# A fused attention and FFN kernel: the halves of the attention products are added by accumulating transfers instead of by GpSimd

## The reference

```python
x = x + _layernorm(attn(_layernorm(x), ...))
x = x + _layernorm(ffn(_layernorm(x), ...))

# attn: rows of x are seen as tokens of C = 16 channels, split in two branches of 8 channels.
# In a branch, windows of 8 tokens attend to each other:
attn = softmax(q * 8 ** -0.5 @ k.T)          # 8 x 8 for each window, hd = 8
out = attn @ v + lepe                        # lepe: 3-tap convolution of v
att = concat([x1, x2]) @ proj_w + proj_b     # then a layer norm over the 16 channels, and + token

# ffn: int8 weights (512 x 2048, 2048 x 512) with scales
gate = silu((x @ w_gate) * s_gate)
up = (x @ w_up) * s_up
y = ((gate * up) @ w_down) * s_down
```

## Time and profile before

| | us |
|---|---|
| median of 2 runs | 1000.54 (999.96 to 1001.12) |
| the profiled execution, its own time | 1001.03 |
| its span, first to last instruction | 999.3 |
| PE busy | 910.1 |
| DVE busy | 825.5 |
| POOL busy | 765.8 |
| ACT busy | 658.6 |
| mean granted clock of TensorE | 0.968 |

### The profile page before, as it was taken

The page is one execution under the profiler, slowest core; times in us unless marked ns, Lnnn a source line. Parts: engine busy times, 40 slices in busy tenths (PEclk is TensorE's granted clock), DMA queues, the critical chain, the costliest instruction groups (busy, mean ns, idle before and its releaser), DMA issues.

```text
span 999.3 us, 17730 instructions
## 1 busy us (share of the span) xinstructions
PE 910.1 (91%) x6511; PEld 705.6 (71%) x6511; DVE 825.5 (83%) x1099; ACT 658.6 (66%) x1153; POOL 765.8 (77%) x698
## 2 busy tenths in 40 slices
PE   1566499989999999999999999999999999989996
PEld 1444387767878777777777787877777787767674
DVE  2799898978898998989898998989898989894322
ACT  1876477676768768586767778586767686654431
POOL 1477686978889797989889797988899787876432
PEclk9878599999999999999999999999999999989998
DMA  7112212040311313040402213040403111120201
GB/s 202 42 43 50 76 26 60 1 128 1 87 41 44 85 22 106 1 127 1 98 30 62 66 33 95 2 128 1 127 1 77 31 43 43 23 64 19 67 11 32
DMA packets 68886, 54.94 MB, mean 55 GB/s; under 512 B 40384, under 2 KB 56768, under 8 KB 68800
## 3 DMA queue, kind: packets, MB, share of 16 engines
q1 hardware_dynamic: 63936, 53.49, 20.0%
q10 hardware_dynamic: 4864, 0.32, 0.3%
HBM read 37.02 MB, written 16.78 MB: 54 GB/s over the span
## 4 chain that ended last, share of the span: by engine, by line
PE 76%; DVE 10%; POOL 5%; issue 3%; DMA 2%; ACT 2%; SPq 1%; POOLq 0%; DVEq 0%; ACTq 0%
PE ps_up L552 21%; PE ps_gate L552 19%; PE ps_acc L571 18%; PE ps_w L513 10%; PE ps_w L533 3%; PE ps_w L504 2%; POOL sum L808 2%; DVE fst L1033 2%; DVE xr L1028 2%; PE ps_w L543 2%; DVE prod L950 1%; PE ps_w L522 1%; DMA xrow<-in_L_attn_x 1%; DVE mid L1049 1%; SPq L432 1%
## 5 line engine op out<-in xcount | busy, mean ns | idle before, releaser
L808 POOL TENSOR_TENSOR sum<-prod 128x1024 f32<-128x1024 f32 x128 | 301.7, 2366 | 46.4 <-DVE prod L950 39.2
L950 DVE TENSOR_TENSOR prod<-ps_x,qkvl 128x2048 f32<-128x2048 f32 x128 | 291.3, 2279 | 5.0 <-ACT ps_x L664 4.6
L571 PE MATMUL ps_acc<-wd,mid 128*128 128x512 f16 x1024 | 241.4, 379 | 0.0
L552 PE MATMUL ps_gate<-xhi,wg 128*128 128x256 f16 x1024 | 233.6, 275 | 3.0 <-DVE xlo L1040 3.0
L552 PE MATMUL ps_up<-xhi,wu 128*128 128x256 f16 x1024 | 232.3, 274 | 1.6 <-DVE mid L1049 1.6
L552 PE MATMUL ps_gate<-xlo,wg 128*128 128x256 f16 x1024 | 233.6, 275 | 0.0
L552 PE MATMUL ps_up<-xlo,wu 128*128 128x256 f16 x1024 | 232.1, 274 | 0.0
L732 ACT ACTIVATE mid<-ps_gate,sgate 128x256 f32<-128x256 f32 x256 | 107.1, 470 | 170.0 <-PE ps_gate L552 169.5
L876 POOL TENSOR_TENSOR mid<-mid 128x512 f16<-128x512 f32 x128 | 148.7, 1162 | 52.4 <-ACT mid L738 52.4
L1049 DVE SCALAR_TENSOR_TENSOR mid<-ps_up,sup,mid 128x256 f32<-128x256 f32 x256 | 110.1, 471 | 91.2 <-PE ps_up L552 69.2
L571 PEld LDWEIGHTS ps_acc<-wd,mid 128*128 128x128 f16 x1024 | 100.3, 98 | 96.7
(11 more groups left out here) (138 smaller groups left out, 1279.6 us busy)
## 6 DMA issues: line engine op xcount, KB each, us to landing
xrow<-in_L_attn_x SPq DMA_DIRECT2D x16, 512.0 KB, 4.5
xb<-in_L_attn_x SPq DMA_DIRECT2D x128, 64.0 KB
attn_rows<-ratt SPq DMA_DIRECT2D x32, 256.0 KB, 2.6
o<-attn_rows SPq DMA_DIRECT2D x32, 256.0 KB, 3.5
xr<-in_L_attn_x SPq DMA_DIRECT2D x16, 512.0 KB, 5.0
out_x<-y SPq DMA_DIRECT2D x15, 512.0 KB, 5.3
mid<-in_L_ffn_w_gate SPq DMA_DIRECT2D x1, 1024.0 KB, 5.4
mid<-in_L_ffn_w_up SPq DMA_DIRECT2D x1, 1024.0 KB, 8.1
```

The costliest lines, as they stand in the source:

```text
L552: mm = nc.tensor.matmul(ps[:, ROWS * i:ROWS * i + ROWS], w[:, k, P * j:P * j + P], xs[:, n % 2, k, :], start=(k == 0 and part == 0), stop= ...
L571: return nc.tensor.matmul(ps_acc[q][:], f[:, m % SPLITS, ROWS * i + P * q:ROWS * i + P * q + P], wd[:, 2 * m + i, :], start=(m == 0 and pa ...
L808: nc.gpsimd.tensor_tensor(sum4[:, u % 2, :].rearrange("p (s c) -> p s c", c=4), s[:, :, 0:4], s[:, :, 4:8], ALU.add).then_inc(half_done, 1)
L950: nc.vector.tensor_tensor(prod[:, half].rearrange("p (s j k) -> p s j k", j=WIN, k=WIN), left[:, :, None, :].broadcast_to([P, 4 * WIN, WIN ...
```

## The change

- `halve` is no longer a GpSimd addition. GpSimd issues a transfer that adds the second half of a product buffer onto the first, inside SBUF: 128 partitions, 1024 float32 (4 KB) each, so 512 KB read, 512 KB added to. Its end is signalled by the transfer's semaphore.
- For that, VectorE writes the products in another layout: the first four of each eight in the first half of the buffer, the last four in the second. The reduction reads the first half. `sum4` is gone.
- There are three product buffers (`RING = 3`). A product waits for the sum of the unit three before, no longer for the GpSimd addition of the unit two before.
- In `finish`, ScalarE copies the two accumulators out of PSUM (`finish_copy`), and GpSimd multiplies them by the scales (`finish_scale`); VectorE only takes the statistics. The last tile's `finish_last` stays as it was.
- `START`, `PLAN` and `OWN` have new contents.

```diff
-        prod = sb("prod", [P, 2, 4 * WIN * WIN * HB])
-        sum4 = sb("sum4", [P, 2, 1024])
+        prod = sb("prod", [P, RING, 2, 1024])
...
+            def finish_copy(n, bank):
+                act.wait_ge(down_done, CHUNKS * n + CHUNKS)
+                need(act, s_out, 16 * n)
+                for q in range(2):
+                    nc.scalar.activation(y[:, q, :], ps_acc[q][:], ACT.Copy).then_inc(acc_read, 1)
...
             def halve(n, u, stage):
-                pool.wait_ge(prod_done, 2 * UNITS * n + UNITS * stage + u + 1)
-                need(pool, sum_done, 2 * UNITS * n + UNITS * stage + u - 1)
-                s = prod[:, u % 2, :].rearrange("p (s c) -> p s c", c=HB)
-                nc.gpsimd.tensor_tensor(sum4[:, u % 2, :].rearrange("p (s c) -> p s c", c=4), s[:, :, 0:4], s[:, :, 4:8],
-                                        ALU.add).then_inc(half_done, 1)
+                unit = 2 * UNITS * n + UNITS * stage + u
+                pool.wait_ge(prod_done, unit + 1)
+                parts = prod[:, unit % RING]
+                pool.dma_start(parts[:, 0], parts[:, 1], accum_op=ALU.add).then_inc(half_done[unit % RING], 16)
...
+            def finish_scale(n, bank):
+                if n == 0:
+                    pool.wait_ge(scales_set, 1)
+                pool.wait_ge(acc_read, 2 * n + 2)
+                for q in range(2):
+                    nc.gpsimd.tensor_tensor(y[:, q, :], y[:, q, :], sdown[:], ALU.mult).then_inc(y_scaled, 1)
...
             def products(n, u, stage):
                 br, half = u // 2, u % 2
-                need(dve, half_done, 2 * UNITS * n + UNITS * stage + u - 1)
+                unit = 2 * UNITS * n + UNITS * stage + u
+                need(dve, sum_done, unit + 1 - RING)
...
-                nc.vector.tensor_tensor(prod[:, half].rearrange("p (s j k) -> p s j k", j=WIN, k=WIN),
+                nc.vector.tensor_tensor(prod[:, unit % RING].rearrange("p i (s k) -> p s i k", k=4),
...
             def reduce_unit(n, u, stage, dst):
-                dve.wait_ge(half_done, 2 * UNITS * n + UNITS * stage + u + 1)
-                nc.vector.tensor_reduce(dst, sum4[:, u % 2, :].rearrange("p (s c) -> p s c", c=4), AX.X,
+                unit = 2 * UNITS * n + UNITS * stage + u
+                dve.wait_ge(half_done[unit % RING], 16 * (unit // RING) + 16)
+                nc.vector.tensor_reduce(dst, prod[:, unit % RING, 0].rearrange("p (s c) -> p s c", c=4), AX.X,
                                         ALU.add).then_inc(sum_done, 1)
...
             def finish(n, bank):
-                dve.wait_ge(down_done, CHUNKS * n + CHUNKS)
-                need(dve, s_out, 16 * n)
-                for q in range(2):
-                    nc.vector.tensor_tensor(y[:, q, :], ps_acc[q][:], sdown[:], ALU.mult).then_inc(acc_read, 1)
-                dve.wait_ge(acc_read, 2 * n + 2)
+                dve.wait_ge(y_scaled, 2 * n + 2)
```

More of the change, by code:

```diff
@@ L42 @@
 TERMS = 96
+RING = 3
 Bank = namedtuple("Bank", "ps last")
@@ L194, in sandwich_kernel @@
         prod_done = sem("prod_done")
-        half_done = sem("half_done")
+        half_done = [sem(f"half_done_{i}") for i in range(RING)]
         sub_done = sem("sub_done")
@@ new lines, in sandwich_kernel @@
+        PLAN = [(-111.23, ("load_row",)), (-89.34, ("stats",)), (-86.02, ("load_xb",)), (-74.99, ("spread",)),
+                (-69.59, ("apply",)), (-66.23, ("xt", 0, 0)), (-62.34, ("xt", 0, 1)), (-61.16, ("qkv", 0, 0)),
+                (-56.61, ("qkv", 0, 1)), (-56.43, ("qkv", 0, 2)), (-55.04, ("qkv", 0, 3)), (-54.12, ("xt", 1, 0)),
+                (-53.12, ("qkv", 1, 0)), (-50.99, ("qkv", 1, 1)), (-48.63, ("xt", 1, 1)),
+                (-48.41, ("token_bias",)), (-48.19, ("qx", 0)), (-47.89, ("qkv", 1, 2)), (-44.29, ("qkv", 1, 3)),
+                (-43.63, ("qk", 0)), (-43.27, ("qx", 1)), (-40.79, ("qk", 1)), (-40.70, ("qk", 2)),
+                (-40.50, ("qk_sum", 0)), (-37.81, ("qk_sum", 1)), (-35.59, ("qk", 3)), (-35.22, ("softmax", 0)),
+                (-34.06, ("qk_sum", 2)), (-33.65, ("exp", 0)), (-32.21, ("pv", 0)), (-30.32, ("qk_sum", 3)),
+                (-30.24, ("softmax", 1)), (-29.00, ("pv_sum", 0)), (-27.30, ("exp", 1)), (-26.98, ("pv", 1)),
+                (-26.09, ("pv", 2)), (-25.60, ("att_store",)), (-25.03, ("pv", 3)), (-24.55, ("pv_sum", 1)),
+                (-22.51, ("recip",)), (-22.28, ("pv_sum", 2)), (-21.30, ("attn_out",)), (-20.25, ("pv_sum", 3)),
+                (-17.36, ("cat", 0)), (-16.74, ("cat", 1)), (-16.58, ("proj", 0)), (-16.16, ("square", 0)),
+                (-15.84, ("cent_var",)), (-15.83, ("load_xr",)), (-15.40, ("proj", 1)), (-15.01, ("square", 1)),
+                (-14.95, ("cent_std",)), (-13.82, ("cent_out",)), (-5.85, ("ffn_norm1",)), (-3.54, ("norm1_add",)),
+                (-3.00, ("ffn_norm2",)), (-2.78, ("norm2_apply",)), (-1.96, ("fx", 0)), (-1.07, ("fx", 1)),
+                (5.99, ("keep_x1",)), (31.56, ("finish_scale",)), (32.08, ("finish_copy",)), (34.00, ("finish",)),
+                (39.66, ("finish_apply",)), (40.11, ("finish_add",))]
@@ L373, in order @@
                     step = (name, n, *rest)
-                    if step not in placed and not (n == TILES - 1 and name in ("finish", "finish_apply", "finish_add")):
+                    if step not in placed and not (n == TILES - 1 and name.startswith("finish")):
                         put(3 * CHUNKS * n + place, step)
@@ L769, in _ @@
                   "norm2_apply": norm2_apply, "keep_x1": keep_x1, "fx": fx, "gate": gate, "fuse_hi": fuse_hi,
-                  "finish_apply": finish_apply, "finish_apply_last": finish_apply_last, "cast": cast})
+                  "finish_copy": finish_copy, "finish_apply": finish_apply, "finish_apply_last": finish_apply_last, "cast": cast})
         @block.gpsimd
```

168 lines of the change are left out of this document (82 added, 86 removed), and 6 rows, old and new, of tables (OWN, START).

## The result

The changed kernel takes **1049.98 us**, the median of two runs (1047.85 and 1052.11), against 1000.54: a ratio of 1.0498, 95% interval 1.0458 to 1.0537. It is 5% slower; the forecast was 993. The profiled execution spans 1050.3 us, that of before 999.3.

What follows compares the result with a forecast made beforehand. The start was taken as bound by attention steps mostly on VectorE, the rest by TensorE. Span 999.3 + 3.0 (start) - 10.3 (gaps) = 992.0, with 1.2 for execution over span: 993 us, range 979 to 1018.

Steps and rivals of the forecast that it cites:

- 0.6 is hidden: Middle tiles: VectorE's stalls on transfers come to 0.6 us a tile, hidden in its room of 6.2 us.
- Nothing for that: Start, SyncE: tile 0's residual load, behind nine row loads, lands just in time; 0 us, up to 3 in the range.
- gone, 5.9: Ahead of tile 14's first gate: 4.4 us of gaps and 1.5 of slow clock vanish, as VectorE has 4.8 less there.
- Part 1, L = 5.5: GpSimd's additions become transfers: latency L from issue to landing taken as 5.5 us, bounds 2.6 and 9.0.
- a rival for a held-up issue: Each issue waits out one VectorE instruction, at most 2.28 us, making latency 7.8: 1017 us; chance 0.08.
- Part 2, latency over cover: Middle: a sum stalls VectorE by latency beyond its work between product and sum (cover, smallest 5.2 us); 0.6 a tile.
- wrong in kind: Sign set beforehand: TensorE idles in every tile, or products take other than about 2.3 us.
- The rival's 0.15: Transfer latency over the cover, deciding at 7.6 us: at 9.0, 8.6 us a tile, about 1115 us; chance 0.15.
- The moved scaling: Finish: ScalarE's wait for the last down and GpSimd's in finish_scale are both hidden; no cost to the end.
- Part 3, the start: Start, step by step: first softmax 1.4 us ahead, attn_out 4.5 behind, first gate at 120.3, 3.0 us behind.
- Part 4, the gaps: TensorE's gaps: 4.4 us at 221.77 (late residual load) and 5.9 ahead of tile 14's first gate vanish; gain 10.3.
- down by some 265: GpSimd's busy time falls by some 265 us (301.7 less 15 x 2.4), without effect on the end.

Runs made afterwards that it cites:

- e14: Kernel before (old order, VectorE scaling) with three buffers, new product layout and transfers cut to 16 of 1024 numbers a partition, rest unadded: 1003.7 us.
- e18: Kernel before (old order, VectorE scaling) with three buffers, new product layout and transfers of 512 of 1024 numbers a partition, rest unadded: 1023.9 us.
- e2: Kernel before (old order, VectorE scaling) with full accumulating transfers, new product layout and three buffers: 1101.8 us, ratio 1.1009.
- e13: Changed kernel with each transfer cut from 1024 to 16 numbers a partition (8 KB), rest unadded: 1028.3 us.
- e4: Changed kernel with VectorE scaling the down projection's result again, transfers kept: 1066.6 us.
- e7: Changed kernel with VectorE scaling again and GpSimd adding the halves instead of transfers; new order and three buffers stay: 1060.5 us.
- e8: Kernel before, old order, with scaling moved to ScalarE and GpSimd; GpSimd adds the halves in place, in three buffers: 1032.3 us.
- e16: Changed kernel with GpSimd additions of only 16 of 1024 numbers instead of transfers, rest unadded; new order and moved scaling stay: 1017.9 us.
- e9: Changed kernel with TensorE's second projection and ScalarE's square put back to their earlier places, copy, scaling and statistics behind them: 1058.5 us.
- e10: Changed kernel with the last finish_apply and finish_add moved forward, so that the residual's next load is issued sooner: 1065.6 us.
- e11: Changed kernel with token_bias early, no own places for tiles 14 and 15, projection and square put back, last apply and add forward: 1078.9 us.
- e12: Old order, GpSimd adding, scaling on ScalarE and GpSimd (1032.3 us), with ScalarE's copy put behind the second square and VectorE's statistics later: 1063.5 us.
- e3: Changed kernel with token_bias of tile 0 moved early in START, ahead of tile 0's second softmax: 1047.5 us.
- e15: Changed kernel with a third buffer for the residual rows, whose load waits for the addition of three tiles back: 1082.3 us.

## Why the prediction was wrong

The forecast was a gain of 7 us, the result a loss of 49. What failed most are three terms that were put at nothing or at a gain: the stalls on transfers ("0.6 is hidden"), the loads in the start ("Nothing for that") and the places of tiles 14 and 15 ("gone, 5.9"). By the prediction's own steps, with the 51.1 us of the marks as the whole:

- **Part 1, L = 5.5.** Near for a transfer by itself (4.6 to 5.1 from issue to landing), and the product kept its length (2277 ns). Mis-sized where it mattered: a product's transfer is issued when GpSimd's queue comes to it (2.4 us late in the tile shown, and for two of the eight products of a middle tile), and there it lands in 6.35 us beside other transfers: 8.8 in all. I had a rival for a held-up issue, but by a port and one VectorE instruction; the queue ahead of the issue, which I could have counted in the new order, I did not.
- **Part 2, latency over cover.** That a sum stalls VectorE by what its latency exceeds its cover by is shown (e14, e18, e2), and the covers came within 0.5 us (by e13's timeline 7.5 and 7.5 for the first and fourth of the score stage; 5.3, 7.1, 6.2 and 4.7 for the second stage). The stalls were mis-sized: 0.6 us a tile forecast, 2.7 measured. "So 0.6 is hidden" is the failed sentence. VectorE's room, which I took as the bound below which stalls are free, is borne out in the old order only: there VectorE scales, so it is 54.6 - 49.8 = 4.8 us by my own numbers, and the tiles of e18 begin to grow between 4.1 and 4.9. In the new order the room was to be 6.2, the waits are 2.7, and still full transfers make the tile 0.8 us longer than short ones (57.28 against e13's 56.52). Which sum it is that isn't free is not shown by itself; the longest waits of a middle tile are those of the fourth score sum, 1.4 us in the mean, which a softmax stands behind. TensorE stands 1.6 us a tile, which is wrong in kind by my own words, though these were loose: it stood 0.4 in every tile before. The rival's 0.15, with 8.6 us a tile, was right for the old order in its direction and not for the new one.
- **The moved scaling, "both hidden. It costs the end nothing".** Not shown as a term by itself in the new order, as e4 and e7 get slower without it. In the old order it costs 32 us (e8). I had named who waits and what is queued behind, and then called it hidden without asking whether `cent_var`, behind that queue, had slack (it waits 2.95 us there, 0.91 before).
- **Part 3, the start.** The steps up to `cent_var` came within 1.4 us: first product 35.3 (34.4), first maximum 46.7 (45.6), `attn_out` 73.0 (74.3), `cent_var` 84.9 (86.2), `scales` 2.7 us without its hold (3.5). Then "Nothing for that", said of SyncE: the first gate came at 126.3, not 120.3. I priced the residual's load there and not `token_bias` of tile 0, which the order moved behind `attn_out`, nor the loads that wait for it. With short transfers the first mark is at 113.7, as before, so it took both: late issue, and slow issue beside the transfers.
- **Part 4, the gaps.** The one near tile 2 shrank: tile 1 to 2 takes 57.9, before 59.6, so 1.7 of my 4.4. The other I had "gone, 5.9": instead the new places of tiles 14 and 15 made tile 13 12.9 us late, 12.1 of them with short transfers too. I counted two steps moved out of VectorE's way and not what the other places written for tiles 14 and 15 did to the tile ahead (TensorE stands 3.8 us for `rmask` and 3.5 at the mark).
- **GpSimd "down by some 265", without effect on the end.** Down by 150, as 128 issues take 115.1 us of it, 0.91 each; without effect, as said.

The balance, by the marks of the profiled executions of the change and of e13: of 51.1 us, 27 go with the transfers' size (9.1 in the start, 14 to tile 12, 4 after it), and 24 stay with short ones (7 to tile 12, 12 in tile 13, 5 after). By the medians of all runs it is 22 and 28; the profiled execution of the change lies 2.1 us above its median and that of e13 3.3 below, so the parts of the balance hold to some 5 us in all. What stays open: how the 0.6 to 0.9 us a tile that the new order costs with short sums (e16, e13) divide between the moved scaling and the places, since every part was tuned into the order and e9 to e12 only disturbed it.

## What to carry to other kernels

Work taken off an engine that nothing waits for was worth nothing here, while its replacement's latency counts: from the producer's end, through the issuing engine's queue, to the landing beside the other traffic. So count the queue ahead of each issue, and don't take an engine's mean free time for slack at a given sum. In an order fitted to its durations a wait in the profile is no price: of six edits that removed or shortened a wait which the trace showed, one came out 2.5 us faster, which the intervals don't tell from nothing (e3), and five lost 8 to 32 us (e9 to e12, e15). So move a step only with all that waits behind it, and expect a load issued earlier to meet other transfers. To price one part of a change that also brings a new order, shrink that part's duration in both orders rather than undo it.
